# Attention outputs normalised with features on partitions, a float32r LoRA product, merged placement transfers and a new instruction order

## The reference, cut to what matters

```python
qkv = layer_norm(x) @ w_qkv.T                 # 87 x 768 per image
q, k = rope(layer_norm(q)), rope(layer_norm(k))
o = softmax(q @ k.T / 4) @ v                  # 16 heads of 16
h = x + o @ w_proj.T + b_proj
y = layer_norm(h)
w = top2(softmax(y @ gate_w.T))               # 8 experts
out = h + y @ W_lin.T + b_lin + sum_e w[e] * (y @ left[e]) @ right[e]
```

## Time and profile before

| what | us |
|---|---|
| median of three runs | 742.79 (741.1 to 745.35) |
| span of the profiled execution, first to last instruction | 734.0 |
| what lies around the span, by the median | 8.8 |
| PE busy in the span | 673.9 |
| DVE busy | 531.2 |
| POOL busy | 491.0 |
| ACT busy | 432.0 |

### The profile page before, as it was taken

How to read it: one execution, slowest core, us unless ns; L and a number is a source line. 1 busy time by engine, 2 the same in 40 slices (tenths; PEclk the granted TensorE clock), 3 DMA queues, 4 the chain that set the end, 5 groups by cost and what they waited for, 6 DMA issues and landing times.

```text
span 734.0 us, 24407 instructions
## 1 busy us (share of the span) xinstructions
PE 673.9 (92%) x9431; PEld 564.8 (77%) x9431; DVE 531.2 (72%) x1192; ACT 432.0 (59%) x1115; POOL 491.0 (67%) x564
## 2 busy tenths in 40 slices
PE   5998998999985799999999999999999999999873
PEld 3987887888853577888888888888888888887652
DVE  2468687887978646788878878878878887866642
ACT  4553452635442346677777676677776777776541
POOL 3667563764648428787877877876976977975442
PEclk9999999999996969999999999999999999999996
DMA  8963472231011223223232332332332332122001
GB/s 222 237 163 116 129 224 47 54 83 44 22 24 40 59 54 79 63 70 82 67 78 73 75 83 73 79 82 72 78 83 68 79 86 67 42 54 62 26 25 34
DMA packets 69528, 58.73 MB, mean 80 GB/s; under 512 B 30607, under 2 KB 68646, under 8 KB 69286
## 3 DMA queue, kind: packets, MB, share of 16 engines
q1 hardware_dynamic: 69414, 57.18, 30.9%
HBM read 33.69 MB, written 11.40 MB: 61 GB/s over the span
## 4 chain that ended last, share of the span: by engine, by line
PE 71%; DVE 12%; issue 4%; ACT 4%; SPq 3%; POOL 3%; DMA 2%; POOLq 0%; DVEq 0%; ACTq 0%
PE p_a L1355 13%; PE p_c L1355 10%; PE p_conv L758 8%; PE p_kv L758 7%; PE p_o L1427 6%; PE p_s L1415 5%; PE p_mm L758 4%; PE p_s L1397 4%; PE p_n L1435 3%; PE p_c L1474 3%; PE p_a L1381 3%; PE p_s L1411 2%; DVE t L1282 2%; DMA kr<-qkT 2%; DVE kv L656 1%
## 5 line engine op out<-in xcount | busy, mean ns | idle before, releaser
L1291 DVE TENSOR_REDUCE mx<-p_s 87x16 bf16<-87x1392 f32 x64 | 102.5, 1602 | 44.6 <-PE p_s L1397 44.4
L1214 ACT ACTIVATE prT<-p_s 87x1392 f32<-87x1392 f32 x64 | 85.2, 1331 | 29.3 <-PE p_s L1415 27.8
L1121 POOL TENSOR_TENSOR t<-t,ss_rs 116x512 f32<-116x512 f32 x48 | 50.9, 1060 | 58.9 <-ACT ss_rs L1190 57.8
L426 POOL TENSOR_TENSOR xs_lo<-xcols,xs_hi 120x585 fp32r<-120x585 f32 (+1 forms) x45 | 60.4, 1348 | 43.7 <-ACT xs_hi L483 43.7
L1415 PE MATMUL p_s<-qr,kr 32*87 32x87 f32 x2048 | 68.8, 257 | 0.0
L1115 POOL TENSOR_TENSOR t<-t 116x512 f32<-116x512 f32 x48 | 62.4, 1299 | 5.6 <-DVE t L1282 5.6
L1135 POOL TENSOR_TENSOR yT_lo<-y_raw,yT_hi 128x232 fp32r<-128x232 f32 x48 | 32.5, 678 | 47.1 <-issue 31.4
L1124 POOL TENSOR_TENSOR t<-t,tabs 116x512 f32<-116x512 f32 x48 | 61.2, 1276 | 2.7
L1415 PEld LDWEIGHTS p_s<-qr,kr 32*87 32x87 f32 x2048 | 60.3, 154 | 0.0
L1411 PE MATMUL p_s<-mxT,pick_row 32*87 32x87 bf16 x1024 | 55.7, 208 | 1.9 <-ACT mxT L1208 1.9
L1427 PE MATMUL p_o<-prT,vp 87*32 87x87 f32 x2048 | 55.1, 248 | 0.1
(11 more groups left out here) (287 smaller groups left out, 2077.8 us busy)
## 6 DMA issues: line engine op xcount, KB each, us to landing
xcols<-in_x_cols SPq DMA_DIRECT2D x12, 822.7 KB, 8.1
h<-h_tokens SPq DMA_DIRECT2D x16, 348.0 KB
out<-out_sb SPq DMA_DIRECT2D x48, 116.0 KB
h_tokens<-in_txt SPq DMA_DIRECT2D x4, 1232.0 KB, 8.7
x<-in_txt_cols SPq DMA_DIRECT2D x32, 154.0 KB, 4.1
qr<-qkT SPq DMA_DIRECT2D x64, 58.0 KB, 2.0
kr<-qkT SPq DMA_DIRECT2D x64, 58.0 KB, 2.0
vp<-vt SPq DMA_DIRECT2D x32, 87.0 KB
```

Of the source, the lines that this page charges most:

```text
L426: nc.gpsimd.tensor_tensor(xs.lo[:, n % XS_SLOTS, :, 0:M].bitcast(F32R), raw, xs.hi[:, n % XS_SLOTS, :, 0:M], ALU.subtract).then_inc(S['xs_ ...
L1214: nc.scalar.activation(prT[:, k % 2], p_s[0:SEQ, :, 0:QUADS * SEQ], ACT.Exp, scale=HD ** -0.5).then_inc(S['s_exp'], 1)
L1291: nc.vector.reduce_max(mx[:, k % 2, :, 0:QUADS], p_s[0:SEQ, :, 0:QUADS * SP].rearrange("p j (a k) -> p j a k", k=SP)[:, :, :, 0:SEQ], AX_X ...
```

## The change

1. **Normalising.** Values are written by ACT straight into a layout with ones between them (`vt` and `vp` are `[HD, 2, HEADS]`), so numerator and sum of a feature fall on neighbouring partitions of `p_o`. After the copy to `oT`, SP issues four DMAs per image (step `part`) that line up numerators and sums in `parts` on 128 partitions. DVE then takes a reciprocal of 128x174 sums and multiplies 128x174 numerators, both inputs in SBUF. The result has features on partitions, so `oN` and `oB` and the copy of L1225 are gone; ACT makes the high part and GpSimd the remainder from `on`. The rows of `w_proj` are permuted on the host to fit.
2. **LoRA.** DVE writes three copies of the weighted activations, one instruction per tile. PE transposes three times, ACT rounds to `twT`, DVE forms a remainder in 32 of its rows (new step `tw_lo`, 32x348), and `lora` is one float32r matmul of 98 rows per tile.
3. **Placement.** `qr` and `kr` become one tensor `strips`; two DMAs take the place of eight. The DMAs of `values` move twice the bytes, as the ones travel along.
4. **PSUM.** `proj`, `yT` and `ffn` of tile 1, the LoRA transpose and the second `lora` use `p_n`, which `oN` and `oB` had.
5. **Order.** All step tables are new.

```diff
+        strips = sb("strips", [P, 2, 2, 4, GT + 2])
-        vp = sb("vp", [SEQ, 2, GB, 2 * HD, HEADS])
-        vt = sb("vt", [TP, 2, TILES, C])
+        vp = sb("vp", [SEQ, 2, GB, HD, 2, HEADS])
+        vt = sb("vt", [TP, 2, TILES, HD, 2, HEADS])
-        LAST_BANK = {'tile': 'ACA', 'gate': 'A', 'lora': 'CA'}
+        TILE_BANKS, LAST_BANKS = {'tile': 'CNC', 'gate': 'N', 'lora': 'CN'}, {'tile': 'ACN', 'gate': 'A', 'lora': 'CN'}
...
-                    for a in range(QUADS):
-                        r = slice(64 * (a % 2), 64 * (a % 2) + 64)
-                        sp.dma_start(qr[0:P:2, half, a, c0:c1], qkT[r, half, a // 2, c0:c1]).then_inc(k_in[half][k], 16)
-                        sp.dma_start(kr[0:P:2, half, a, c0:c1], qkT[r, half, 2 + a // 2, c0:c1]).then_inc(k_in[half][k], 16)
+                    for side in range(2):
+                        sp.dma_start(strips[0:P:2, half, side, :, c0:c1], qkT[64 * side:64 * (side + 1), half, :, c0:c1]).then_inc(k_in[half][k], 16)
+                if name == 'part':
+                    n4 = GB * g + k + 1
+                    sp.wait_ge(S['o_out'], n4)
+                    wait(sp, S['o_norm'], n4 - 2)
+                    for side in range(2):
+                        for n in range(2):
+                            sp.dma_start(parts[side:P:2, k % 2, n], oT[n:P:2, k % 2, side:4:2]).then_inc(o_in[k % 2], 16)
...
                 if name == 'oT':
                     wait(act, S['pv'], n4)
-                    wait(act, S['oN'], n4 - 2)
+                    wait(act, o_in[k % 2], 64 * ((n4 - 1) // 2))
                     nc.scalar.copy(oT[:, k % 2], p_o[:, 0:4 * SEQ].rearrange("p (c q) -> p c q", c=4)).then_inc(S['o_out'], 1)
-                if name == 'oB':
-                    wait(act, S['oB'], n4)
+                if name == 'on':
+                    wait(act, S['o_norm'], n4)
...
-                    nc.scalar.copy(on_raw[:, k % 2], p_n[:, 0:CC * SP].rearrange("p (c q) -> p c q", c=CC)[:, :, 0:SEQ])
...
                 if name == 'norm':
-                    dve.wait_ge(S['oN'], n4)
-                    wait(dve, S['oB'], n4 - 2)
-                    o3 = p_n[0:SEQ, :].rearrange("p (h e) -> p h e", e=2 * HD)
-                    link(nc.vector.reciprocal(rd[:], o3[:, :, HD]))
-                    nc.vector.tensor_tensor(on[:, k % 2].rearrange("p (h d) -> p h d", d=HD), o3[:, :, 0:HD],
-                                            rd[:].unsqueeze(2).broadcast_to([SEQ, HEADS, HD]), ALU.mult).then_inc(S['o_norm'], 1)
+                    dve.wait_ge(o_in[k % 2], 64 * ((n4 + 1) // 2))
+                    wait(dve, S['on_low'], n4 - 2)
+                    link(nc.vector.reciprocal(rd[:, k % 2], parts[:, k % 2, 1]))
+                    nc.vector.tensor_tensor(on[:, k % 2], parts[:, k % 2, 0], rd[:, k % 2], ALU.mult).then_inc(S['o_norm'], 1)
...
+                    shape = [TP, 3, EXPERTS, RANK]
+                    for tile in range(TILES):
+                        last = nc.vector.tensor_tensor(
+                            tw[:, tile].rearrange("p (n e r) -> p n e r", n=3, r=RANK),
+                            f[:, half, tile, C:C + LR].rearrange("p (e r) -> p e r", r=RANK).unsqueeze(1).broadcast_to(shape),
+                            g_w[:, tile].unsqueeze(1).unsqueeze(3).broadcast_to(shape), ALU.mult)
+                    last.then_inc(S['tw_ok'], 1)
+                if name == 'tw_lo':
+                    dve.wait_ge(S['twT_out'], g + 1)
+                    lows = slice(LR, 2 * LR)
+                    nc.vector.tensor_tensor(twT[lows].bitcast(F32R), product('gate', g, k)[lows, 0:GT].rearrange("p (t n) -> p t n", t=TILES),
+                                            twT[lows], ALU.subtract).then_inc(S['tw_low'], 1)
...
-                if name == 'oN':
-                    use('N', S['o_norm'], n4)
-                    pe.wait_ge(S['o_out'], n4)
-                    for c in range(4):
-                        mm_ = nc.tensor.transpose(p_n[0:SEQ, c * P:(c + 1) * P], oT[:, k % 2, c], ident[:])
-                    mm_.then_inc(S['oN'], 1)
-                if name == 'oB':
...
                     for n, tile in enumerate(LORA_TILES[k]):
-                        mm_ = nc.tensor.matmul(product('lora', g, k)[0:TP, n * C:(n + 1) * C], twT[:], right[:, tile], start=True, stop=True)
+                        mm_ = nc.tensor.matmul(product('lora', g, k)[0:TP, n * C:(n + 1) * C], twT[:, tile].bitcast(F32R),
+                                               right_3[:].bitcast(F32R), start=True, stop=True)
...
-GROUP_SP = table("""cols.0.-400 rows.0.-440 place.0.210 values.0.258 place.1.291 values.1.438 store.0.1111 store.1.1115 store.2.1253""")
-GROUP_PERIOD, GROUP_START = 276, 2100
+GROUP_SP = table("""rows.0.-36597 cols.0.-29897 place.0.17637 place.1.19661 values.0.37015 part.0.41459 values.1.42053 part.1.45420
+                part.2.46349 part.3.59141 store.0.120419 store.1.122983 store.2.124437""")
```

More of the change, by code:

```diff
@@ L1013, in attention_ffn @@
         k_in = [[consts.loads[f"k_in{half}{n}"] for n in range(2)] for half in range(2)]
+        o_in = [consts.loads[f"o_in{n}"] for n in range(2)]
         stored = consts.stored
@@ L1082, in clear_strips @@
                 pool.wait_ge(W['conv'], CONVS)
[L1083 removed]
+                for part in (strips, mx):
                     ready(nc.gpsimd.memset(part[:], 0.0))
@@ L1303, in step @@
                     dve.wait_ge(S['hb_ok'], n3)
+                    if g == 0 and k == 0:
+                        for part in range(2):
+                            dve.wait_ge(W[f'st_rows{part}'], ROWS_OUT * len(range(part, STEPS, 2)))
                     nc.vector.tensor_tensor(h2[:, half, k], product('tile', g, k)[0:TP, 0:C], hb[:, k], ALU.add).then_inc(S['h2_ok'], 1)
```

227 lines of the change are left out of this document (115 added, 112 removed).

## The result

The changed kernel takes 924.42 us (median of four runs, 920.41 to 925.26). The kernel before took 744.07 us beside it. The ratio is 1.2431, with a 95% interval of 1.2364 to 1.2497. I had forecast 755 us and a range of 728 to 781. The sign was right, but the time lies 143 us outside the range.

The account below looks back on a forecast made before the run. The prediction took DVE, with its waits for GpSimd, to bound the changed kernel at 29.3 us a group. The span 734.0 + 13.5 - 1 = 746.5 us, plus 8.8 to the median, gave 755 us, range 728 to 781.

Parts of the forecast that it names:

- The bound before, PE: Steady stage of the kernel before: PE busy 27.96 us of a 28.26 us group, so PE bounds it.
- PE's work after, 24.9 us a group: PE in the changed kernel: dropped `oN`, `oB` and cheaper LoRA products take 3.0 us off 27.96 a group.
- The reciprocal, 1065 ns: DVE's normalising: 128x174 sums at 5.2 ns an element, 1065 ns against 244, +3.3 us a group.
- The waits behind GpSimd: DVE's multiply and weighting, both inputs in SBUF, wait for POOL's instructions: 1.7 us a group.
- forecast need of 28.9: DVE after the change: 27.25 us of work plus 1.7 of waits for POOL, 28.9 us a group.
- Rival 5, eight times a plain element: DVE's reciprocal at 7.5 ns an element, 1459 ns: 1.6 us more a group, 776 us in all; chance 0.05.
- Idle time of 0.4 us beside a full DVE: Steady stage: DVE as bound engine still idles 0.4 us a group, making the period 29.3 us.
- hidden, apart from what it delays: SP's issuing stays at about 17 to 19 us a group, hidden; the output's latency costs nothing in the steady stage.
- forecast period of 29.3 us: Steady stage bound by DVE: 29.3 us a group, +1.04 on 28.26, 13 times, +13.5 us.
- Rival 4, a new loop: SP's `parts` wait for DVE's normalising, delaying placement, strips and `peak`: period 31.2, 780 us; chance 0.13.
- The merged placement: SP's placement falls from 16 to 4 issues a group, about 0.6 us each; landing takes 2.0 us.
- LoRA: PE saves 0.84 us a group, two transposes add 0.2; DVE gains 0.4 for weighting and 0.5 for `tw_lo`.

Follow-up runs that it names:

- y_no_values_recip: Changed kernel with value transfers cut at multiples of 16 partitions and issued early, then left out from the third group on, and no reciprocal: 740.5 us.
- x_no_values: Changed kernel with value transfers cut at multiples of 16 partitions and issued early, then left out from the third group on; reciprocal kept: 781.2 us.
- u_paired: Changed kernel with value transfers cut at multiples of 16 and early, four buffers, and `parts` DMAs issued for two blocks at once (8 per group, not 16): 902.9 us.
- d_before_place: Kernel before with only the merged placement, two DMAs instead of eight: 736.4 us, ratio 0.991 to 1.001.
- q_cut_narrow: Changed kernel in its own order, each value transfer cut in two at partition counts sharing no large factor (41, 29, 23 and rest): 1073.7 us.

## Why the prediction was wrong, point by point

- **The bound before, PE.** Right as a reading of the earlier trace rows.
- **PE's work after, 24.9 us a group.** Nearly right. In `y_no_values_recip` PE is busy for 229.87 of 250 us at a period of 28.3: 26.0 us at a clock of 0.98.
- **The reciprocal, 1065 ns.** It took 1226 (median), the multiply 520 against 331 plus a wait of 350 to 400, the weighting 251 and `tw_lo` 514 against 495:

```profile
L1319 DVE RECIPROCAL rd<-parts x64: 1219/1226/1242, 277.8 to 891.0; 128x174 f32<-128x174 f32 x64
```

```profile
L1320 DVE TENSOR_TENSOR on<-parts,rd x64: 340/520/1164, 279.1 to 892.2; 128x174 f32<-128x174 f32 x64
```

```profile
L1357 DVE TENSOR_TENSOR tw<-f,g_w x48: 245/251/722, 354.3 to 912.9; 116x96 f32<-116x96 f32 x48
```

```profile
L1365 DVE TENSOR_TENSOR twT<-p_n,twT x15: 512/514/514, 360.4 to 899.1; 32x348 fp32r<-32x348 f32 x15
```

  That is (1226 - 176)/171 = 6.1 ns an element beyond the third, not the 5.2 of the earlier trace rows, and 0.6 us a group more. The waits behind GpSimd were smaller than priced (the median multiply is 0.19 us above 331 ns): GpSimd was busy for 55% of the stalled stage (273.77 of 500 us) and not for the 79% that I took, and the prediction's own working gives 0.55 x 0.82/2 = 0.23 us with it. The two errors cancel by luck: DVE is busy for 360.62/500 x 40.3 = 29.1 us a group, against a forecast need of 28.9.
- **Rival 5, eight times a plain element.** It had 1459 ns; the trace has 1226, nearer to the 1065 of the line of the rows. The rival came from the Trainium skill, VectorE: DVE Perf Modes, section "First, the fixed hardware budget", which gives the reciprocal a repeat count of 8; that this makes it eight times a plain element was my estimate, and the trace does not bear it out (6.1 against 0.94 ns an element).
- **Idle time of 0.4 us beside a full DVE: undersized.** The one kernel in which DVE is the bound, `x_no_values`, shows 31.2 us a group for 29.2 us of DVE work (234.30/250), so 2.0. A floor of DVE work is not a period when PE needs nearly as much and both are in order. 1.6 us times 13 groups are 21 of the 26 us between 755 and its 781.
- **SP, "hidden, apart from what it delays": this step failed.** I counted SP's time per group (17 to 19 us) and compared it with the period. What it delays was the question, and I followed it for strips alone. The same paragraph let the latency of the output path cost nothing; `u_paired` shows that it is on a loop once DVE waits for `parts` ahead of a rotation. In the changed kernel 21% of the chain is SP's issuing.
- **The values had no term at all.** The diff moved `values.0` in SP's table from ahead of `place.1` to behind `part` steps and doubled the bytes of a row, and the front part of this document shows both. Neither got a price. Order and DMA engines of these transfers are 127 of the 180 us, and taking the rest of them away gives another 16, or 54 once the reciprocal is gone too. This is the error that decided: the forecast period of 29.3 us was that of a DVE-bound stage, and the stage was bound by a loop of 40.3 us through SP's queue and a landing of 10.3 us that the sum did not contain.
- **Rival 4, a new loop.** It named the right kind of thing, SP's `parts` with what is queued behind them, and the clock that falls with idle PE (0.84 in the stretch, against 1.00). But its loop went through strips, for which PE waited once in the whole changed kernel (3.6 us), and was priced from today's 2.27 us before the maxima. The loop that closed went through the values, with a landing of 10.3 us in it.
- **The merged placement.** Right in the issue, with a median of 637 ns, and no change can be told in `d_before_place`. The landing was taken as the 2.0 us of one of the eight; it is 3.6 us in `d_before_place` and 4.8 in the changed kernel for the first two tiles.
- **LoRA.** Its chain of transposes, copy and `tw_lo` had no term. In the old order the part costs 2.4 us a group, about four times the gain of 0.6 that I had booked.

What stays open: how the 16 us that `x_no_values` gains (54 without the reciprocal) divide between SP's issues and traffic on the DMA engines, and what the LoRA part is worth in the new order by itself.

## What to carry to other kernels

Price every transfer that a diff moves or widens, by its landing and by what it is now queued behind, before any engine's work is summed; on an in-order issuing queue the question is not how full it is but which `wait` stands ahead of which issue. Cut transfers at partition counts with a large common factor up to 16. When taking one suspect away changes nothing, take away two: limits of equal length hide each other, and here one alone brought 2 us, the other 16, and both 57.

## What was not expected of the hardware

- A transfer of 29, 58 or 87 partitions with 2,048 bytes each landed in 10.3 us when four were issued together; with the same rows cut at multiples of 16 it took 2.1 us where the chain shows it. Cutting into as many pieces at 41, 29 and 23 made PE wait up to 15.1 us.
- An issue can take several times its usual length, and in an in-order queue everything behind it waits. SP's issues of `parts` have a median of 608 ns and a maximum of 3,576 in the changed kernel; what held the long ones up no run shows:

```profile
L1084 SPq DMA_DIRECT2D parts<-oT x256: 593/608/3576, 266.1 to 885.8; - x128
```

- The reciprocal on DVE costs 5.2 ns an element between 3 and 16 elements per partition, and 6.1 on average from there to 174.
- The granted clock, an average over a stretch between TensorE's two levels of 1.2 and 2.4 GHz, went down with PE's idle time: 1.00 in the steady stage before, 0.84 after, 0.71 from 350 to 600 us in `q_cut_narrow`. PE's 9,031 instructions are busy for 649.9 us in `y_no_values_recip`, 691.2 in the changed kernel and 746.1 in `q_cut_narrow`. So a stall on a queue costs twice, once as the wait and once as slower work behind it.
